# Moving the DMA that stores the scan's result from SyncE's queue to GpSimd's

## What is computed

```python
xn = _layernorm(x)                                   # x: (4, 4096, 2048)
# branch 1: recurrence
xp = einsum('btd,ed->bte', xn, W_in)
dt = softplus(einsum('bte,he->bth', xp, W_dt) + b_dt)
a  = exp(dt[..., None] * -exp(log_A))                # decay per channel
ys = scan(ys_t = a_t * ys_{t-1} + xp_t)              # over t
y1 = einsum('btd,ed->bte', ys, W_out)
# branch 2: feed-forward, w_* int8, s_* scales
gate = silu((xn @ w_gate) * s_gate); up = (xn @ w_up) * s_up
y2 = ((gate * up) @ w_down) * s_down
return x + y1 + y2
```

## Time and profile before

| | us |
|---|---|
| time, median of the 2 timed runs | 3675.95 |
| the two timed runs | 3622.13, 3729.76 |
| the profiled execution, its own time | 3599.66 |
| its span, slowest core (core 4) | 3598.0 |
| spans of the 8 cores | 3571.7 to 3598.0 |
| mean granted TensorE clock of the cores | 0.966 to 0.968 |

### The profile page before, as it was taken

The page is one execution under the profiler, slowest core; times in us unless marked ns, Lnnn a source line. Parts: engine busy times, 40 slices in busy tenths (PEclk is TensorE's granted clock), DMA queues, the critical chain, the costliest instruction groups (busy, mean ns, idle before and its releaser), DMA issues.

```text
span 3598.0 us, 36876 instructions; the slowest of 8 cores (3571.7 to 3598.0 us)
## 1 busy us (share of the span) xinstructions
PE 3241.0 (90%) x15088; PEld 1460.4 (41%) x15088; DVE 480.9 (13%) x544; ACT 537.3 (15%) x772; POOL 193.3 (5%) x286
## 2 busy tenths in 40 slices
PE   0184798999999999999999999969989997997999
PEld 0031343444444444444444444424433443443444
DVE  3153221000000000000000002200012004003000
ACT  2143332122221111111111111100000000000000
POOL 1000000000000010001000100000000000000000
PEclk9887899999999999999999999989999998998999
DMA  9775342211121112112211222266566557556553
GB/s 187 115 180 137 63 85 75 71 53 53 54 70 53 53 55 69 53 53 57 67 53 53 58 78 88 77 165 212 181 232 198 179 187 241 179 181 228 175 176 114
DMA packets 157476, 419.01 MB, mean 116 GB/s; under 512 B 84016, under 2 KB 84032, under 8 KB 142208
## 3 DMA queue, kind: packets, MB, share of 16 engines
q1 hardware_dynamic: 112736, 229.67, 20.4%
q0 software_dynamic: 41984, 168.13, 18.1%
q10 hardware_dynamic: 2592, 18.88, 2.0%
HBM read 322.38 MB, written 68.16 MB: 109 GB/s over the span
## 4 chain that ended last, share of the span: by engine, by line
PE 85%; DMA 6%; SPq 4%; DVE 2%; issue 1%; ACT 1%; POOL 0%; ACTq 0%; DVEq 0%; POOLq 0%
PE ps_g L598 25%; PE ps_u L598 25%; PE pso L715 24%; PE pso L709 6%; PE ps_xp L420 5%; SPq L313 4%; DMA wdq_sb<-wd 2%; DMA xtb<-x_full 1%; DVE wdq_sb L544 1%; DMA xn_scr<-xnb 1%; DMA ytb<-ys_scr 1%; PE psdtl L326 1%; DVE xsq_s L259 0%; DVE stats L258 0%; DMA winNb<-winN 0%
## 5 line engine op out<-in xcount | busy, mean ns | idle before, releaser
L715 PE MATMUL pso<-wdq_sb,ftb 128*128 128x512 bf16 x4096 | 923.0, 386 | 61.2 <-DVE wdq_sb L544 61.2
L598 PE MATMUL ps_g<-xnT,wgb 128*128 128x512 bf16 x4096 | 897.2, 380 | 13.7 <-DMA wgb<-wg 13.7
L598 PE MATMUL ps_u<-xnT,wub 128*128 128x512 bf16 x4096 | 894.5, 379 | 0.0
L715 PEld LDWEIGHTS pso<-wdq_sb,ftb 128*128 128x128 bf16 x4096 | 403.7, 99 | 569.7 <-issue 102.4
L598 PEld LDWEIGHTS ps_g<-xnT,wgb 128*128 128x128 bf16 x4096 | 402.0, 98 | 498.4 <-issue 17.5
L598 PEld LDWEIGHTS ps_u<-xnT,wub 128*128 128x128 bf16 x4096 | 400.2, 98 | 483.9
L621 DVE TENSOR_TENSOR fb<-gb,ub 128x512 bf16<-128x512 bf16 x256 | 108.8, 425 | 1562.8 <-ACT ub L613 1562.8
L613 ACT ACTIVATE ub<-ps_u,su_c 128x512 bf16<-128x512 f32 x256 | 175.9, 687 | 707.0 <-PE ps_u L598 707.0
L610 ACT ACTIVATE gb<-ps_g,sg_c 128x512 bf16<-128x512 f32 x256 | 175.9, 687 | 705.3 <-PE ps_g L598 705.3
L709 PE MATMUL pso<-wo_sb,ytb 128*128 128x512 bf16 x1024 | 234.1, 382 | 29.6 <-DMA ytb<-ys_scr 29.6
L420 PE MATMUL ps_xp<-xnT,winTb 128*128 128x512 bf16 (+1 forms) x1280 | 260.7, 364 | 0.0
(11 more groups left out here) (56 smaller groups left out, 514.0 us busy)
## 6 DMA issues: line engine op xcount, KB each, us to landing
ftb<-f_scr SPq DMA_DIRECT2D x64, 2048.0 KB, 8.9
wgb<-wg POOLq DMA_DIRECT2D x64, 512.0 KB, 5.4
wub<-wu POOLq DMA_DIRECT2D x64, 512.0 KB, 6.1
f_scr<-fb POOLq DMA_DIRECT2D x64, 512.0 KB, 5.3
wdq_sb<-wd POOLq DMA_DIRECT2D x32, 1024.0 KB, 16.4
ytb<-ys_scr SPq DMA_DIRECT2D x64, 512.0 KB, 10.0
xtb<-x_full ACTq DMA_DIRECT2D x18, 1024.0 KB, 11.1
winTb<-winT POOLq DMA_DIRECT2D x32, 512.0 KB, 5.8
```

What stands on the lines that cost most here:

```text
L598: inst = TE.matmul(ps[:, cols], wsb[kb][:, dt * P:(dt + 1) * P], xnT[:, dt * T + WU + ch * 512: dt * T + WU + ch * 512 + 512], start=(dt = ...
L715: inst = TE.matmul(ps_o[ko][:, :], ft_b[kf][:, jt * P:(jt + 1) * P], wdq_sb[:, jt * QW:(jt + 1) * QW], start=False, stop=(jt == NJ - 1))
```

## The change

The wait for the cast, the wait for the buffer's previous spill and the spill's DMA itself are issued from GpSimd's queue instead of SyncE's. Source, destination, shape and semaphores of the DMA are the same, and so is its place in the order of the code: in GpSimd's queue it now stands between the `winT` load of tile gi+2 and that of tile gi+3.

```diff
             c_ybf.inc(inst)
-            SY.wait_ge(c_ybf.h, c_ybf.n)
+            GP.wait_ge(c_ybf.h, c_ybf.n)
             if p2 == 0:
                 tt0, nblk, col0 = 0, 6, WU
             else:
                 tt0, nblk, col0 = 6, 10, 0
-            r_dys.refill(SY, k2)
-            r_dys.inc(SY.dma_start(out=ys_scr[tt0:tt0 + nblk, :, et2, :]
+            r_dys.refill(GP, k2)
+            r_dys.inc(GP.dma_start(out=ys_scr[tt0:tt0 + nblk, :, et2, :]
                                    .rearrange("t p c -> p t c"),
                                    in_=ybf_b[k2][:, col0:col0 + nblk * P]
                                    .rearrange("p (t c) -> p t c", c=P)), k2)
```

## The result

| | before | changed |
|---|---|---|
| time, median over all executions (31 and 32) | 3695.44 | 3582.17 |
| lowest | 3593.27 | 3577.65 |
| the profiled execution | 3599.66 | 3584.59 |
| its span, slowest core | 3598.0 (core 4) | 3582.7 (core 1) |
| mean span of its 8 cores | 3583.6 | 3574.2 |

Of the others the ratio is 0.9942, 95% interval 0.9928 to 0.9957: some 21 us (15 to 26) faster. A repeat beside other executions of before gave 0.9959 (0.9945 to 0.9973), 15 us (10 to 20). Part of the 21 us are three times of before, 3618.81, 3622.13 and 3624.02, which stand some 17 us and more above its others (3593.27 to 3602.11).

What follows compares the result with a forecast made beforehand. TensorE's feed-forward work was three quarters of the span; the gain lay in scan-stage holes. -18.7 + 1.1 = -17.6 us on 3599.66 gives 3582.1; midway to 3604.6, with the smaller offset, gives 3594, range 3567 to 3690.

Steps and rivals of the forecast that it cites:

- the sum: Whole kernel: 18.7 us gained before chunk 4, 1.1 lost at the last spill, -17.6 us, giving 3582.1.
- the number: Forecast time of 3594, midway between 3582.1 and 3604.6, the latter with the smaller timed-run offset added.
- the cost that was put at nothing: GpSimd's winT loads go out later behind the spill's wait; the third weight buffer covers it, cost zero.
- where the wait was and that it would go: SyncE's spills delay chunk 4's transposes; without them the 17.29 us TensorE hole closes, next tile 18.7 us earlier.
- my own sign: TensorE's hole before chunk 4's matmuls would be under 1.5 us.
- The other sign: SyncE's queue: the prediction is wrong if a transpose's issue stands longer than 2 us after 356.
- Rival A: Transposes of chunks 3 and 4, now without pause, or their landing are slowed: half the gain or none; chance 0.14.
- The end: Last spill, in the open before the first gate matmul, lands later from GpSimd: 1.1 us lost (0 to 2.3).
- 2.8 either way: Before 300 us, spills share a queue with winT and service order may move: 2.8 us either way, value 0.
- The offset: Timed runs stood 22 and 130 us above the profiled one; some such offset was expected for the changed kernel.
- Rival B: Pass 1: winT loads come late because GpSimd sits in a wait, once over 18.4 us from issue; slower, chance 0.04.
- held the shared port pair: Pass 1: a scan on VectorE shuts GpSimd out of writing descriptors; spill and load up to 2.2 us later.

Runs made afterwards that it cites:

- e3: Kernel before, all spills still on SyncE, with chunk 4's transposes issued right behind chunk 3's, ahead of spills 10 and 11; 0.9950 of before.
- e1: Changed kernel with each spill on GpSimd's queue issued behind the next winT load instead of ahead of it; 0.9957 of before.
- e5: Kernel before with all spills issued from ScalarE's queue, behind its own cast, instead of SyncE's; 0.9974 of before.
- e2b: Kernel before with only spills 10 and 11 moved to GpSimd, on semaphores of their own; 0.9957 of before.
- e4: Kernel before with only the wait for the cast added on GpSimd, spills staying on SyncE; 1.0006 of before.
- e7: Kernel before, spills on SyncE, transposes of chunks 2, 3 and 4 issued behind tiles 4, 8 and 10 instead of 8, 10 and 12; 0.9910 of before.
- e10: e7's early transposes, chunk 3's and 4's matmuls behind tiles 12 and 15, spills on GpSimd behind the next winT load; 0.9947 of before.

## Why the prediction was right or wrong

Two steps failed. The one that made the forecast wrong is the last, from the sum to the number. The other is the cost that was put at nothing, and it is the one to learn from.

**Right: where the wait was and that it would go.** Transposes of chunks 3 and 4 in one row of 32; first gate matmul earlier; no TensorE wait for `winT`. (The start of the first gate matmul moves with tile 0, so it is read from the stretches.) e3 shows that the order in SyncE's queue was the cause, and e1 and e3 together that it was worth what the sum had for it: chunk 3 to the last xp fell from 225.4 to 205.5 and 205.0, 20 us, against the forecast 18.7. The excess of 1.3 us is about what the clock explains: before, the tile behind the hole was slowed too on five of the eight cores (8.5 to 8.9 us against 7.08, 1.0 us at the mean), and I had counted only the 16 matmuls. Behind a hole of 0.97 us or less these took 1.91 us, the full level of 2.4 GHz (e1, e3); behind the 4.02 us on core 1 of the changed kernel they took 3.57, and the tile behind them 9.08.

**Wrong: "cost: nothing, covered by the third weight buffer".** I priced the late load by who waits for the load, and nobody does. What it does to others I didn't ask: its bytes move to a time at which a store and the last transposes are on the chain. That is two terms I had at zero. Chunk 2 to 3: +5.7 us in the profile, +4.6 in the repeat. Of that 4.1 and 3.7 are the store of tile 17, landing in 6.0 to 8.6 us instead of 3; the rest is chunk 3's transposes, a little slower to issue and land. Chunk 4: the last transpose lands in 5 to 8 us on seven cores instead of 2.4 to 4, which leaves a hole of 2.7 us (mean of the cores) and with it the low clock; of the 20 us only 15.3 arrive, 16.2 in the repeat. By my own sign, a hole under 1.5 us before chunk 4's matmuls, this failed on six of the eight cores. (The other sign, no issue of a transpose over 2 us, failed on five, but it also fails in e1 and e3, which lose nothing; it was a poor sign.) Rival A named load 15 and spill 11 as company for the transposes, with a loss of 9 us where chunk 4 lost 4.7; the store of tile 17 it did not name. It stood at 0.14, and I let the 20.93 us of the old transposes speak against it: that row shows the time to issue them, not the landing of the last.

**The end: right in kind.** 1.1 us was forecast, 1.9 and 1.4 measured, inside 0 to 2.3. The landing, 3.9 to 5.3 us, has my 4.1 near its lower edge. What I left out is 0.5 us between the cast's end and the issue: 0.6 on GpSimd (572.76 to 573.35) and 0.1 on SyncE (588.24 to 588.35). The estimate from the first-byte figures of the Trainium skill, "DMA: Bandwidth & Descriptors", section "Specifications", was 0.4; the measured loss is several times that.

**The number was the step that failed.** The sum was -17.6 us, 0.5%. Measured are -21 (15 to 26) for the slowest core in the first comparison, or -15.7 without the three high times of before, -14.2 in the second, and -12.4 for the mean of the cores. So the sum was too large by 2 to 5 us. The stretches sum to -8.6 and -12.6: the two terms left out, near 5 us each, are there, against them the 1.3 us of clock and, in the repeat, 2.4 us before chunk 2, where I had 2.8 either way and the value 0.

But I gave 3594, against a time before of 3675.95, which reads as a gain of 82 us, 2.2%, over four times my own sum, while my chances had 0.93 for a change within 2%. I had seen that the two timed runs stood 107 us apart with the profiled one below both. I added the gain to the profiled execution, put 12 us on top that no row explains, and set this against a median that rests on other executions. The offset was a guess about which executions would be shown, and the changed kernel needed none of it.

That its median of 3582.17 is the sum (3582.1) to a tenth is luck: the profiled execution I started from stands 2 to 4 us above the mean of the others before, and the gain was too large by about as much. A forecast of the difference, taken from rows, should have been laid on one base for both kernels, and said so.

**GpSimd and the scans.** Rival B didn't happen. `winT` loads in pass 1 landed in 5.4 to 8.2 us on the eight cores (5.1 to 8.1 before), far from 18.4. The issue of a spill takes 0.85 us for 768 pieces and up to 0.99 for 1280, near the 0.8 taken. Most of pass 1's spills are issued under a scan, here one with the scan from 433.47 to 436.35 (GpSimd, then VectorE, core 1):

```profile
435.09 0.98 POOL L475 DMA_DIRECT2D ys_scr<-ybfb  x1 [7.90 <-ACT ybfb L466]
436.06 0.55 POOL L366 DMA_DIRECT2D winTb<-winT  x1
```
```profile
433.47 2.88 DVE L447 TENSOR_TENSOR_SCAN ysb<-ab,state_s,xpsb 128x1280 f32<-128x1280 f32 x1 [7.50 <-ACT xpsb L435]
```

It neither waits for the scan's end nor takes notably longer than the last one, issued beside none (0.95). Had the scan held the shared port pair, the case for which I had drawn on the Trainium skill, "SBUF — State Buffer", section "Who interferes with whom", the issue would have begun at 436.35 and not at 435.09; these scans don't shut GpSimd out.

## What to carry to other kernels

A wait added in front of a load is paid for in two places: who waits for the load, and what the load meets when it comes later. Look for stores and last transfers on the chain close to the new time: here 1.75 and 2.6 us were too close, and 4.7 us cost nothing.

When a queue holds back something urgent, first try to reorder that queue: one moved line (e3) gave more than moving 32 DMAs to another engine, which also took a late load and a slower last spill into the bargain. Keep plain loads ahead of anything that waits (e1, e5).

Give a forecast as a difference, worked out from rows, and state the base that both kernels are laid on. A median of two runs 3% apart is no base for a change of 0.5%.

## What the runs showed of the hardware

The landing of a 512 KB store depended steeply on how far ahead of it a 512 KB load was issued: 4.7 us ahead 2.7 to 3.8 us (before, e1, e3, e2b), 2.6 us ahead 4.2 to 6.4 (e4), 1.75 us ahead 6.0 to 8.6 (changed and its repeat). In all of these a spill of 192 KB stood 2.6 to 3.1 us ahead as well.

The 16 transposes of chunk 3 or 4 took 20.2 to 23.7 us to issue in the kernel before, the changed one and e1 to e5. Those of chunk 2 among the loads of rows took 24 to 30 us in e7 and 34 to 56 in e10. Their cost is no constant.
